# Twelve weight halves cut by GpSimd late and waited for per tile, a shorter scatter chain, and three held units instead of two

## What is computed

```python
x = x + tanh(g_xattn[0]) * xattn(layernorm(x), ctx_1024, mask, W, b)     # x is 2 x 1024 x 256, 77 context rows
x = x + tanh(g_ffn[0])   * ffn(layernorm(x), w_router, fc1_w, fc2_w, gate_w, up_w, down_w)

def ffn(x, ...):                                   # 2048 tokens, H = 256
    logits = x @ w_router                          # 8 experts
    top_logits, top_idx = top_k(logits, 2)
    scores = softmax(top_logits)
    for e in range(8):                             # fc1_w[e] is 256 x 512, fc2_w[e] is 256 x 256
        proj, gate = split(permuted_e @ fc1_w[e])
        out_e = silu(proj) * gate @ fc2_w[e]
    moe = sum of the two experts' rows, weighted by scores
    shared = silu(x @ gate_w) * (x @ up_w) @ down_w    # 256 -> 512 -> 256
    return moe + shared
```

## Time and profile before

| what | us |
|---|---|
| time, median of 3 runs (lowest to highest) | 241.2 (240.91 to 241.91) |
| the profiled execution's own time | 239.41 |
| its span in the profile | 237.7 |
| PE busy over the span | 220.1 (93%) |
| DVE busy | 172.4 (73%) |
| ACT busy | 130.0 (55%) |
| POOL busy | 123.5 (52%) |

### The profile page before, as it was taken

How to read it: one execution, slowest core, us unless ns; L and a number is a source line. 1 busy time by engine, 2 the same in 40 slices (tenths; PEclk the granted TensorE clock), 3 DMA queues, 4 the chain that set the end, 5 groups by cost and what they waited for, 6 DMA issues and landing times.

```text
span 237.7 us, 5259 instructions
## 1 busy us (share of the span) xinstructions
PE 220.1 (93%) x1413; PEld 192.5 (81%) x1413; DVE 172.4 (73%) x513; ACT 130.0 (55%) x316; POOL 123.5 (52%) x176
## 2 busy tenths in 40 slices
PE   7688999999899999889799999999999999999980
PEld 7588899978687888768688888888888888887860
DVE  1878897797568899996967656656656656655795
ACT  2565888772747644445226556556556556555320
POOL 1797796554868887888401334334334344344600
PEclk9999999999999999999999999999999999999997
DMA  5999940000132125322242433333333432108876
GB/s 148 295 397 407 398 163 3 0 0 25 45 110 74 67 92 201 124 81 92 68 121 60 134 115 93 108 114 93 99 119 89 117 97 68 49 26 296 271 270 265
DMA packets 18131, 32.05 MB, mean 135 GB/s; under 512 B 3046, under 2 KB 9323, under 8 KB 18104
## 3 DMA queue, kind: packets, MB, share of 16 engines
q1 hardware_dynamic: 14096, 22.28, 29.5%
q0 software_dynamic: 3408, 8.46, 9.6%
q10 hardware_dynamic: 600, 0.97, 1.3%
HBM read 19.95 MB, written 12.67 MB: 137 GB/s over the span
## 4 chain that ended last, share of the span: by engine, by line
PE 45%; POOL 8%; issue 6%; DVE 3%; DMA 2%; ACT 0%; SPq 0%; DVEq 0%; POOLq 0%
PE bank L977 38%; POOL rows L384 6%; PE bank L1221 4%; PE bank L1241 4%; POOL ew_lo L243 2%; DMA rows<-hrows,slot 1%; DVE acc L949 1%; DMA hrows<-rows 1%; DVE acc L698 1%; DVE act_lo L626 0%; SPq L280 0%; DVE act L912 0%; ACT act_hi L439 0%; ACT act L577 0%; DVEq L62 0%
## 5 line engine op out<-in xcount | busy, mean ns | idle before, releaser
L426 POOL DMA_INDIRECT parts<-y_out,dst x39 | 38.8, 995 | 71.1 <-DVE dst L906 67.5
L912 DVE TENSOR_TENSOR act<-act,bank 128x256 f32<-128x256 f32 x39 | 16.4, 421 | 34.4 <-ACT act L577 32.6
L384 POOL DMA_INDIRECT rows<-hrows,slot x32 | 34.2, 1069 | 12.3 <-issue 12.1
L577 ACT ACTIVATE act<-bank 128x256 f32<-128x256 f32 x39 | 15.0, 384 | 37.4 <-PE bank L977 37.4
L977 PE MATMUL bank<-ew_hi,m_xt_hi 128*128 x78 | 30.9, 396 | 0.1
L977 PE MATMUL bank<-ew_hi,m_xt_lo 128*128 x78 | 30.8, 395 | 0.0
L977 PE MATMUL bank<-ew_lo,m_xt_hi 128*128 x78 | 30.7, 394 | 0.0
L977 PE MATMUL bank<-ew_hi,act_hi 128*128 x78 | 25.2, 323 | 0.2 <-DVE act_lo L626 0.2
L439 ACT ACTIVATE act_hi<-act 128x512 fp32r<-128x512 f32 x16 | 10.1, 631 | 24.0 <-DVE act L685 24.0
L977 PE MATMUL bank<-ew_hi,act_lo 128*128 x78 | 21.9, 281 | 0.0
L977 PE MATMUL bank<-ew_lo,act_hi 128*128 x78 | 21.9, 281 | 0.0
(11 more groups left out here) (179 smaller groups left out, 653.1 us busy)
## 6 DMA issues: line engine op xcount, KB each, us to landing
ew_raw<-in_chunks SPq DMA_DIRECT2D x12, 512.0 KB, 10.7
hrows<-rows SPq DMA_DIRECT2D x39, 130.0 KB, 2.2
low_buf<-parts SPq DMA_DIRECT2D x4, 512.0 KB, 4.8
high_buf<-parts SPq DMA_DIRECT2D x4, 512.0 KB, 4.4
acc<-in_x SPq DMA_DIRECT2D x7, 256.0 KB, 4.8
sw_raw<-in_chunks SPq DMA_DIRECT2D x3, 512.0 KB, 8.5
out<-acc SPq DMA_DIRECT2D x3, 512.0 KB, 2.7
rows<-pad_rows SPq DMA_DIRECT2D x9, 130.0 KB
```

The source lines that it names most:

```text
L384: pool.indirect_dma_start(out=rows, out_offset=bass.IndirectOffsetOnAxis(ap=slot[:, h, k, i:i + 1], axis=0), in_=hrows[:, HT * h + i, :], ...
L426: pool.indirect_dma_start(out=parts, out_offset=bass.IndirectOffsetOnAxis(ap=dst[:, t:t + 1], axis=0), in_=y_out[:, t % SLOTS, :], in_offs ...
L577: a.activation(act[:, p, 0:I], M_H[p][:, 0:I], ACT.Silu).then_inc(s["m_sil"], 1)
L912: TT(act[:, p, 0:I], act[:, p, 0:I], M_H[p][:, I:2 * I], ALU.mult).then_inc(s["m_prod"], 1)
```

## The change

- POOL cuts 20 of the 30 low halves: positions 0 to 7 early, and all twelve chunks of experts 4 to 7, three of them (`MID`) among the scatters and nine (`LAST`) behind the last scatter. DVE keeps ten.
- PE waits ahead of the tiles only for POOL's first eight. A table `t_need` gives for each tile the count of `chunk_lp` that its expert needs, 3e - 1 and at least 8; for the first eight tiles PE loads the entry and waits for it, and at tile 8 it waits for all 20.
- The scatter chain on POOL: `rstd_second(6)` and `(7)` become one call for both groups, the weight fields of half 1 go to DVE, and three cuts stand in it instead of five. ACT's `norm_second(6)` and `(7)` follow behind `silu(2)`, and PE has `down(1)` ahead of `turn_h(6)` and puts `gate(3)` and `up(3)` around `router(6)` and `turn_h(7)`.
- `HELD` is 3: unit 13 moves from ahead of the tiles to the end. The PSUM banks of the tiles' products swap with it.
- 14 instead of 10 warm-up products at the start.

```diff
-IN_A = 7
-HELD = 2
+IN_A = 8
+HELD = 3
 U0 = UNITS - HELD
-MID = tuple(IN_A + 2 * i for i in range(5))
-LAST = tuple(range(CHUNKS - 3, CHUNKS))
-LATER = {3: 1, 4: 1, 5: 1, 6: 1, 7: 1, 8: 1, 9: 2, 10: 2, 11: 2, 12: 3}
+LATE = tuple(range(SCH + 8, SCH + 8 + 3 * (E // 2)))
+MID, LAST = LATE[:3], LATE[3:]
+CHECKED = 8
+LATER = {3: 1, 4: 1, 5: 1, 6: 1, 7: 1, 8: 1, 10: 2, 11: 2}
...
         BP = (bank[1], bank[7])
-        M_H, M_Y, M_A, M_X = (bank[2], bank[3]), (bank[4], bank[7]), bank[1], bank[0]
+        M_H, M_Y, M_A, M_X = (bank[0], bank[1]), (bank[4], bank[7]), bank[3], bank[2]
...
-            def rstd_second(g):
-                pool.wait_ge(s["mean2"], g + 1)
-                sl = slice(GT * g, GT * g + GT)
-                rstd("2", sl, ve2, mv2, nm2, rs2).then_inc(s["pow2"], 1)
-                pool.wait_ge(s["pow2"], g + 1)
-                pool.tensor_tensor(out=nb2[:, sl], in0=nm2[:, sl], in1=rs2[:, sl], op=ALU.mult).then_inc(s["rstd2"], 1)
+            def rstd_second(g, m=1):
+                pool.wait_ge(s["mean2"], g + m)
+                sl = slice(GT * g, GT * (g + m))
+                rstd("2", sl, ve2, mv2, nm2, rs2).then_inc(s["pow2"], m)
+                pool.wait_ge(s["pow2"], g + m)
+                pool.tensor_tensor(out=nb2[:, sl], in0=nm2[:, sl], in1=rs2[:, sl], op=ALU.mult).then_inc(s["rstd2"], m)
...
-            weight_fields(0)
-            scatter(0, 0, 1)
-            rstd_second(NG - 2)
-            scatter(0, 1, 3)
-            rstd_second(NG - 1)
-            scatter(0, 3, 8)
+            weight_fields_first()
+            scatter(0, 0, 5)
+            rstd_second(NG - 2, 2)
+            scatter(0, 5, 11)
             cut_lo(pool, MID[0])
-            scatter(0, 8, 12)
+            scatter(0, 11, 2 * HT)
+            scatter(1, 0, 5)
             cut_lo(pool, MID[1])
-            scatter(0, 12, 2 * HT)
+            scatter(1, 5, 11)
             cut_lo(pool, MID[2])
-            weight_fields(1)
-            scatter(1, 0, 6)
-            cut_lo(pool, MID[3])
-            scatter(1, 6, 11)
-            cut_lo(pool, MID[4])
             scatter(1, 11, 2 * HT)
...
                 a.wait_ge(chunk_in[i // 2], 16)
-                if i == IN_A:
+                if i == SCH + 6:
                     after(a, "mt_ps", NG)
                 if i == CHUNKS - 4:
-                    after(a, "tiles_known", 3)
+                    after(a, "tiles_known", 4)
                 hi(chunk_bufs(i)[1], chunk_bufs(i)[0], "chunk_h")
...
             turn_h(NG - 4)
+            cut_hi(IN_A - 1)
             copy_eT(NG - 1)
             weight_tanh(0)
             silu(0)
             turn_h(NG - 3)
-
-            norm_second(NG - 2)
+            for i in range(IN_A, IN_A + 2):
+                cut_hi(i)
             silu(1)
             silu_hi(0)
+            silu_hi(1)
+            silu(2)
+            cut_hi(IN_A + 2)
+
+            norm_second(NG - 2)
+            norm_second(NG - 1)
             turn_h(NG - 2)
-            silu_hi(1)
-
-            norm_second(NG - 1)
-            silu(2)
+            silu_hi(2)
             turn_h(NG - 1)
-            silu_hi(2)
-            i = IN_A
+            i = IN_A + 3
             for n in range(3, U0 - 1):
                 if n == 5:
                     weight_tanh(1)
                 silu(n)
-                more = 3 if n < 6 else 2
+                more = 3 if n < 8 else 2 if n in (9, 10) else 0
                 for j in range(i, i + more):
...
             softmax_in(NG - 1)
             second_choice(0)
             weigh(0)
+            turn_h(NG - 4)
+            slots(0, bank[7])
             residual(NG - 2)
-            turn_h(NG - 4)
             turn_e(NG - 1)
-            slots(0, bank[7])
             turn_h(NG - 3)
             stats_second(NG - 2)
...
-            turn_h(NG - 2)
             product_lo(1)
             product(2)
+            turn_h(NG - 2)
+            product_lo(2)
             turn_h(NG - 1)
-            product_lo(2)
-
+
+            def weight_fields_last():
+                sl = slice(HT, NT)
+                after(v, "w_tanh", NH)
+                TS(hrows[:, sl, D + 2], wsm[:, 3, sl], tgh[:, 0:1], tgh[:, 0:1], ALU.mult, ALU.add)\
+                    .then_inc(s["fields_last"], 1)
+                TS(hrows[:, sl, D + 3], wsm[:, 3, sl], tgh[:, 1:2], None, ALU.mult).then_inc(s["fields_last"], 1)
+
+            after(v, "tg_half", 2)
+            product(3)
             read_logits(1)
             first_choice(1)
-            product(3)
+            product_lo(3)
             second_choice(1)
-            product_lo(3)
             cut_later(3)
...
+            then(TS(t_needf[:], t_exp[:], float(E - 1), 3.0, ALU.min, ALU.mult), "tb")
+            TS(t_need[:], t_needf[:], -1.0, float(IN_A), ALU.add, ALU.max).then_inc(s["tiles_known"], 1)
...
             add_high(1)
+            product(U0 + 2)
             add_high(2)
+            product_lo(U0 + 2)
             add_high(3)
...
             gate(2)
-            turn_h(NG - 2)
             up(2)
             after(pe, "resid", NT)
             after(pe, "placed", 1)
             down(0)
+            down(1)
+            turn_h(NG - 2)
+            gate(3)
             router(NG - 2)
             turn_h(NG - 1)
-            down(1)
+            up(3)
             router(NG - 1)
-            gate_up(3)
             for n in range(4, U0 - 1):
...
+            def weights_cut(t):
+                if t < CHECKED:
+                    need = pe.value_load(t_need[0:1, t:t + 1], min_val=IN_A, max_val=IN_A + len(LATE))
+                    pe.wait_ge(s["chunk_lp"], need)
+                elif t == CHECKED:
+                    pe.wait_ge(s["chunk_lp"], IN_A + len(LATE))
+
             def weights(e, c, lo_, hi_):
                 return tuple(at(w, 3 * e + c)[:, lo_:hi_] for w in (ew_hi, ew_lo))
 
             def m_up(t, p, e):
                 after(pe, "xT_l", t + 1)
                 after(pe, "m_prod", t - 1)
+                weights_cut(t)
                 mm3(M_H[p][:], lambda k: both(m_xt_hi, m_xt_lo, full_, p, slice(k * P, k * P + P)),
...
             m_turn_x(1, 1)
-            after(pe, "chunk_lp", IN_A + len(MID + LAST))
-            after(pe, "chunk_lv", CHUNKS - IN_A - len(MID + LAST))
+            after(pe, "chunk_lp", IN_A)
+            after(pe, "chunk_lv", CHUNKS - IN_A - len(LATE))
             after(pe, "sil", U0)
-            after(pe, "tiles_known", 3)
+            after(pe, "tiles_known", 4)
             e = [expert_of(0)]
...
             down(U0)
+            gate_up(U0 + 2)
             down(U0 + 1)
+            down(U0 + 2)
 
```

More of the change, by code:

```diff
@@ L234, in by_pool @@
         def by_pool(i):
-            return i < IN_A or i in MID + LAST
+            return i < IN_A or i in LATE
         def chunks_at(slot_):
@@ L274, in _ @@
             after(sp, "scattered", 16 * 2 * NT)
-            after(sp, "tiles_known", 3)
+            after(sp, "tiles_known", 4)
             for t in range(N_TILES):
@@ L773, in cut_later @@
             def cut_later(u):
-                mine = [i for i in range(IN_A, CHUNKS) if i not in MID + LAST]
+                mine = [i for i in range(IN_A, CHUNKS) if i not in LATE]
                 first = sum(m for w, m in LATER.items() if w < u)
@@ L1160, in _ @@
             after(pe, "const_i", 2)
-            for _ in range(10):
+            for _ in range(14):
                 pe.matmul(bank[2][:, 0:P], ident[:], ident[:], start=True, stop=True)
```

14 lines of the change are left out of this document (9 added, 5 removed).

## The result

The changed kernel took 248.1 us (median of 4 runs, 247.84 to 248.35), the kernel before in the same comparison 241.56 us (240.91 to 241.96). The ratio is 1.030, 95% interval 1.026 to 1.035: slower. The forecast was 247.6.

What follows compares the result with a forecast made beforehand. PE was taken as the bound through the tiles. Turn 2.3, clock 2.3 and end 1.8 gave +6.4 us: 245.8 against the profiled 239.4, or 247.6 with the 1.8 to the median carried over; range 237.9 to 250.0.

Steps and rivals of the forecast that it cites:

- Part 1: POOL's scatter chain: last scatter ends at 107.1 us, give or take 1, instead of 111.6.
- Part 2: PE ahead of the turn: 0 to 2 us new waiting before unit 5, 0 to 1 at `rank_first`, not added to the sum.
- Part 3: PE's turn to the tiles: POOL's nine cuts hold DVE to the row's end, so the turn is 2.3 us later.
- the "worse" variant: At the turn `product_lo(10)` falls behind the nine cuts, so `down(10)` too waits: +2.1 us, 249.7 us.
- Part 4: PE behind the standstill: idle 8 us, its clock falls to the lower level, 2.3 us lost, bounds 0 to 3.2.
- Part 5: Behind the tiles: unit 13 adds 4.2 us of PE, DVE's earlier adds save 2.4, net +1.8 us.
- Part 6: Second table load at tiles 0 to 7: taken as 0 us, bounds 0 to 1.8, covered by products queued ahead.
- the first: At the turn DVE gets in at the end of each POOL cut, no clock fall: 238.7 us, chance 0.24.
- The second, as the change is written: At the turn DVE isn't held at all: -4.2 us, 237.0 us, chance 0.08.

Runs made afterwards that it cites:

- experiment 12: Kernel before with 14 warm-up matmuls of PE instead of 10: median 240.01 us, ratio 0.999.
- experiment 1: Changed kernel with the nine cuts moved from the row to one by one behind the first nine result writes: 239.53 us, ratio to before 0.996.
- experiment 2: Changed kernel with the nine cuts in place, POOL waiting behind each for its own end: 240.24 us.
- experiment 3: Changed kernel with five of the nine cuts left in the row and four behind the first four result writes: 242.95 us, ratio to before 1.012.
- experiment 7: Changed kernel with 28 identity matmuls filling PE's standstill ahead of `down(10)`: 247.95 us.
- experiment 4: Changed kernel without the table load and wait of tiles 0 to 7, the wait at tile 8 kept: 245.95 us.
- experiment 6: Changed kernel with 56 identity matmuls put into PE's standstill ahead of `down(10)`: 252.73 us.

## Why the prediction was right, step by step

The direction and the mechanism (VectorE held for the length of the row) were right. That the median came out within 0.5 us (247.6 forecast, 248.1 measured) is in part luck, since the sum holds errors of both signs. Span against span it gave +6.4 us where the traces show +8.9. The 1.8 us by which the profiled execution of the kernel before lay under its median was carried over to the changed kernel, whose profiled execution (248.35) lay at its upper end, 0.25 above its median. Without that carry the forecast would have been 245.8, low by 2.3. By experiment 12 the 1.8 us go with time at the lower clock in most executions of the kernel before. The four runs of the changed kernel have 0.984 to 0.986, which the 6.9 us of its turn at half speed account for (3.4 of 246.6 us are 0.014). So nothing of the kind was there to carry over; which of the edits took it away stays open.

- **Part 1, the scatter chain:** right, though its printed terms for POOL's arrival (55.9, eleven times 1.3, 2.2) give 72.4 and not 72.1. The last scatter ended at 107.66 (107.1, give or take 1), the wait ahead of `MID[0]` was 2.15 us (2.0), and nine cuts took 11.11 us (11.3).
- **Part 2, PE's order:** the waits had their size, but "these don't add up with what follows" was wrong. PE waited 1.0 us for `picked` ahead of unit 5 (the list below) and 1.1 at `rank_first`. A third wait, 1.0 for `product_lo` in unit 10 (102.46), is one of those "in units 9 to 11" that were to go; it stayed. `gate_up(12)` began at 109.60, where the forecast's own rule gives 112.17 - 4.2 = 108.0. PE was 1.6 us late, and so was `product(10)` (105.41 for 103.8). That did not move the turn by itself, but it decided which DVE operation the row of cuts would catch. The first two waits come from cuts too, single ones: `pick`, for which `rank_first` waits, took 1.24 us beside the eighth early cut (51.31 to 52.57) and 0.23 in the kernel before, and one operation on the way to half 1's `picked` took 1.10 instead of 0.22 beside `MID[0]` (75.11 to 76.40). The forecast had the first of these, not the second. From the list of PE's waits from 60 to 112 us, and from DVE's timeline, changed kernel:

```profile
PE bank L1126 <- DVE pick L752: 1.0, 1, 1.0
PE bank L1140 <- DVE act_lo L627: 1.0, 1, 1.0
...
51.42 1.24 DVE L752 TENSOR_TENSOR pick<-oh 128x64 bf16<-128x64 f32 x1
75.39 1.10 DVE L738 TENSOR_TENSOR qa<-lg,mx 128x64 f32<-128x64 f32 x1
```

- **Part 3, the standstill:** that the row holds DVE is shown by experiments 1, 2 and 3. The operation caught was the "worse" variant's: `product_lo(10)`, issued at 107.46, 0.2 us ahead of the first cut's record, instead of a cut behind `product(11)`. Therefore `down(10)` waited too, `down(11)` began at 122.46, 2.0 us behind the 120.5 of the forecast, and the turn was 4.2 us late instead of 2.3 (118.24 in the earlier trace rows). The variant had been priced at 2.1, but not chosen: the forecast had `product_lo(10)` ending at 106.7. With PE 1.6 us late (part 2) it only started at 107.46.
- **Part 4, the clock:** the fall was there, at about 117, 4.5 us after the last product, and lasted until 123.9. The price was wrong: 2.3 forecast, 0.5 to 0.7 measured at the first `m_up`, nothing that can be told in the medians (experiment 7). The term took half of the low stretch as lost, though the sum itself had DVE's chain as what PE waits for; products that run at half speed while PE would wait anyway cost nothing.
- **Part 5, the end:** +2.13 measured, +1.8 forecast. Unit 13 lengthened PE's work behind the last `m_up` from 14.86 to 19.22 us, +4.4 (4.2), and 3.9 us followed the start of the last product (6.1 before), -2.2 (-2.4).
- **Part 6, the table loads:** wrong: 0 taken, bounds 0 to 1.8, 2.2 us measured for the loads with their waits (experiment 4). The argument was that products queued ahead cover a load, taken from the earlier trace rows, where there was one load per `m_up`. With two there are gaps of 0.15 to 0.54 us ahead of tiles 0, 3, 5 and 7.
- **Rivals:** the first (DVE gets in at each cut's end, 238.7 us) is what happens with a pause of 0.08 us (experiment 2: 240.24, of which 1.5 to 2.2 are the loads, which its price had at 0). The second, as the change is written (237.0), is what the same plan gives once the cuts are off the row: 239.53 with the loads, 237.42 with one. Both had their price right and their condition absent: nothing in the changed kernel opened a pause, and nothing kept DVE's reads apart from the row.

Error by error in the span: +2.0 for the caught operation, -1.8 for the clock (-1.6 with 0.7), +2.2 for the loads, +0.3 for the end, together +2.7 against the 2.5 that were missing.

## What to carry to other kernels

Before a row of two-input GpSimd operations is put beside work that matters, look for VectorE operations with two inputs in SBUF in that stretch: in rows of three, five and nine they waited for the end of the row, not of one operation, and the price is the row's length. A wait for its own result behind each GpSimd operation, or other work between them, bounds that price to about one operation. Price a fall of TensorE's clock only for time in which TensorE would not have waited anyway, and count each extra register load with its wait in a loop as a cost on the engine that is never idle. Before an execution's distance from its median is carried over to another kernel, ask what makes it and whether the other kernel has it.

## What the runs showed of the hardware

- GpSimd's back-to-back cuts (128x512, two SBUF inputs, 1.25 us apart) kept VectorE's two-input operation standing for 3.15, 7.02 and 11.88 us with three, five and nine in the row, each time until 0.55 or 0.56 us after the row's end. Pauses of 0.08 us between them were enough to let it in (2.08 us). Beside a single cut a 128x64 operation took 1.24 instead of 0.23 us.
- The exchange costs both: with pauses the nine cuts took 13.91 us instead of 11.11, and single ones 1.63 instead of 1.30.
- Nine one-input GpSimd operations of the same size (TENSOR_SCALAR) took 13.93 us, longer than nine with two inputs, and left VectorE nearly alone (1.31 instead of 0.69 us once).
- A register load with a semaphore wait more per `m_up` on TensorE's queue cost 1.5 us over seven tiles and 0.7 us at the first.
- A 128-column product of the 32-bit identity leaves two records. Their starts lie 0.11 us apart with the clock at its upper level (experiment 6), but 0.21 in the first 5 us (in the earlier trace rows, whose 20 records begin between 1.59 and 5.80). There the clock column says 1.00 (the window below, changed kernel): at the start of these traces the spacing of the products tells the speed, and the column doesn't.

```profile
2.00:4.00 2.00, 2.00 (x11) 2.00 (x11) 0.00 (x0) 0.82 (x1) 0.00 (x0) 1.00 0.55 132
```
